# Turning transfers in attention: query block outermost in `probs` and `pT`, 4 KB runs, four partition groups in turn

## What is computed

```python
def attn(x, ...):                      # x: (1, 2048, 256), 16 heads of 128
    q = x @ (wq_codes * repeat(wq_scales, 32)) + bq      # k, v likewise, to 2048 features
    scores = einsum('bqhd,bkhd->bhqk', q, k) / sqrt(128)
    attn = softmax(scores, axis=-1)
    out = einsum('bhqk,bkhd->bqhd', attn, v)
    return out @ (wo_codes * repeat(wo_scales, 32)) + bo
x = x + layernorm(attn(layernorm(x), ...))
x = x + layernorm(experts(layernorm(x), ...))
```

## Time and profile before

| | us |
|---|---|
| median of 3 runs (lowest, highest) | 2091.43 (2089.87, 2092.95) |
| the profiled execution | 2085.26 |
| its span, first to last instruction | 2083.5 |
| TensorE busy | 1966.5 (94%) |
| VectorE busy | 1750.0 (84%) |
| GpSimd busy | 1525.5 (73%) |
| ScalarE busy | 1417.0 (68%) |
| mean granted TensorE clock | 0.975 of full speed |
| transfers `pT<-probs` | 2032 of 128 KB, 2.3 us to landing in the median |

### The profile page before, as it was taken

How to read it: one execution, slowest core, us unless ns; L and a number is a source line. 1 busy time by engine, 2 the same in 40 slices (tenths; PEclk the granted TensorE clock), 3 DMA queues, 4 the chain that set the end, 5 groups by cost and what they waited for, 6 DMA issues and landing times.

```text
span 2083.5 us, 33186 instructions
## 1 busy us (share of the span) xinstructions
PE 1966.5 (94%) x10902; PEld 1697.1 (81%) x10902; DVE 1750.0 (84%) x2706; ACT 1417.0 (68%) x2686; POOL 1525.5 (73%) x1317
## 2 busy tenths in 40 slices
PE   6999999999999999999999999999999999976882
PEld 5888888888888888888888888888888888865772
DVE  7889889998989888988999898988898898976444
ACT  5777767776777767776777667776777667762444
POOL 2679778887778777977888777977787787973222
PEclk9999999999999999999999999999999999986996
DMA  4667757786767767775767666765677566842443
GB/s 103 158 154 185 177 143 175 176 184 149 169 163 182 164 146 171 176 166 134 167 156 175 151 152 156 179 158 138 161 175 165 137 157 147 205 107 75 131 127 104
DMA packets 238064, 322.66 MB, mean 155 GB/s; under 512 B 47686, under 2 KB 105798, under 8 KB 237894
## 3 DMA queue, kind: packets, MB, share of 16 engines
q1 hardware_dynamic: 234822, 312.15, 63.4%
q0 software_dynamic: 3072, 8.39, 1.3%
HBM read 35.68 MB, written 18.35 MB: 26 GB/s over the span
## 4 chain that ended last, share of the span: by engine, by line
PE 69%; SPq 10%; POOL 6%; ACT 4%; DVE 4%; issue 3%; DMA 2%; another core or an unknown queue 0%; POOLq 0%; ACTq 0%
PE ps_a L749 16%; PE ps_s L621 12%; PE ps_s L622 11%; PE ps_s L623 11%; SPq L395 9%; PE ps_a L750 8%; POOL pT_both L518 5%; PE ps_a L621 3%; PE ps_a L623 3%; PE ps_a L622 3%; ACT probs L1037 2%; DVE part_max L1393 1%; DMA pT<-probs 1%; ACT pT_both L1054 1%; POOL x_rows L594 1%
## 5 line engine op out<-in xcount | busy, mean ns | idle before, releaser
L518 POOL TENSOR_TENSOR pT_both<-pT,pT_both 128x512 fp32r<-128x512 f32 x1016 | 1289.3, 1298 | 342.2 <-ACT pT_both L1054 340.6
L749 PE MATMUL ps_a<-pT_both,v_both 128*128 128x512 f32 x2048 | 743.8, 397 | 1.2 <-POOL pT_both L518 1.2
L1037 ACT ACTIVATE probs<-ps_s,shift 128x1024 f32<-128x1024 f32 x512 | 565.9, 1108 | 259.2 <-DVE shift L1402 258.9
L1054 ACT ACTIVATE pT_both<-pT 128x512 fp32r<-128x512 f32 x1016 | 605.7, 629 | 189.2 <-DMA pT<-probs 157.9
L1418 DVE STREAM_TRANSPOSE probs<-probs 128x1024 f32<-128x1024 f32 x508 | 614.2, 1229 | 58.3 <-ACT probs L1037 57.7
L1393 DVE TENSOR_REDUCE part_max<-ps_s 128x1 f32<-128x1024 f32 x512 | 612.0, 1214 | 19.9 <-PE ps_s L623 18.4
L750 PE MATMUL ps_a<-pT_both,v_both 128*128 128x256 f32 x2048 | 573.9, 280 | 0.0
L749 PEld LDWEIGHTS ps_a<-pT_both,v_both 128*128 128x128 f32 x2048 | 385.3, 188 | 86.6 <-POOL pT_both L518 1.1
L621 PE MATMUL ps_s<-kT_hi,qT_hi 128*128 128x512 f32 x1024 | 406.3, 397 | 15.3 <-ACT probs L1037 12.1
L622 PE MATMUL ps_s<-kT_lo,qT_hi 128*128 128x512 f32 x1024 | 402.9, 393 | 0.0
L623 PE MATMUL ps_s<-kT_hi,qT_lo 128*128 128x512 f32 x1024 | 401.3, 392 | 0.0
(11 more groups left out here) (202 smaller groups left out, 2584.5 us busy)
## 6 DMA issues: line engine op xcount, KB each, us to landing
pT<-probs SPq DMA_DIRECT2D x2032, 128.0 KB, 2.3
x_rows<-zeros SPq DMA_DIRECT2D x46, 128.0 KB, 2.2
xg<-x_rows SPq DMA_DIRECT2D x46, 128.0 KB
y_rows<-y_sb SPq DMA_DIRECT2D x46, 128.0 KB
pT<-in_L_attn_x SPq DMA_DIRECT2D x4, 512.0 KB, 5.7
codes<-in_L_attn_wk_codes SPq DMA_DIRECT2D x16, 128.0 KB, 2.4
scales<-in_L_attn_wk_scales SPq DMA_DIRECT2D x64, 32.0 KB, 3.0
codes<-in_L_attn_wo_codes SPq DMA_DIRECT2D x16, 128.0 KB, 2.3
```

What stands on the lines that cost most here:

```text
L518: pool.tensor_tensor(pT_lo[:, p, :].rearrange("p (i n) -> p i n", i=Q4), pT[:, s % 2, g, :, t:t + 2, :].rearrange("p i t q -> p i (t q)"), ...
L749: nc.tensor.matmul(out_both, v_hi[:, h % 2, k, :], move, start=k == 0, stop=False)
L1037: nc.scalar.activation(out, src, ACT.Exp, bias=shift[:, s % SLOTS, r:r + 1], scale=SCALE, accum_out=sums[:, s % SLOTS, r, g:g + 1])\
L1054: nc.scalar.activation(pT_hi[:, p, :].rearrange("p (i n) -> p i n", i=Q4), pT[:, s % 2, g, :, t:t + 2, :].rearrange("p i t q -> p i (t q)" ...
```

## The change

The index of the block of 32 becomes the outermost in `probs` and in `pT`. In `probs` the order in a partition goes from (g, j, t, r, q) to (j, g, t, r, q), and in `pT` from (g, i, t, q) to (i, g, t, q), where i is the block of 32 queries and j the block of 32 keys within a tile. What a transfer takes from a partition of `probs` and puts into one of `pT` was two runs of 2 KB, one for each g, and is now one of 4 KB. The loops that issue the 16 transfers change too: before, the source group stayed for four transfers while the destination went over the four groups; now four transfers in a row take the sources 0 to 3 and the destinations (i + k) mod 4. The patterns of those that read and write the two tensors follow. The transpose's blocks no longer lie at one distance (j and t can't be joined), so its pattern has one dimension more.

```diff
-        pT = sb("pT", [P, 2, NG2, Q4, GT, RH * 32], f32, att)
+        pT = sb("pT", [P, 2, Q4, NG2, GT, RH * 32], f32, att)
...
-            return probs[:, s % 2, :].rearrange("p (g j t r q) -> p g j t r q", g=NG2, j=Q4, t=GT, r=RH)[:, g]
+            return probs[:, s % 2, :].rearrange("p (j g t r q) -> p j g t r q", j=Q4, g=NG2, t=GT, r=RH)[:, :, g]
...
-                for i in range(Q4):
-                    for b in range(Q4):
-                        src = probs[32 * i:32 * (i + 1), s % 2, :].rearrange("p (g j n) -> p g j n", g=NG2, j=Q4)
-                        dst = pT[32 * b:32 * (b + 1), s % 2, :, i, :, :].rearrange("p g t q -> p g (t q)")
-                        sp.dma_start(dst, src[:, :, b, :]).then_inc(pT_loaded[s % 2], 16)
+                for k in range(Q4):
+                    for i in range(Q4):
+                        b = (i + k) % Q4
+                        src = probs[32 * i:32 * (i + 1), s % 2, :].rearrange("p (j n) -> p j n", j=Q4)[:, b, :]
+                        dst = pT[32 * b:32 * (b + 1), s % 2, i].rearrange("p g t q -> p (g t q)")
+                        sp.dma_start(dst, src).then_inc(pT_loaded[s % 2], 16)
...
-                                   pT[:, s % 2, g, :, t:t + 2, :].rearrange("p i t q -> p i (t q)"),
+                                   pT[:, s % 2, :, g, t:t + 2, :].rearrange("p i t q -> p i (t q)"),
...
-                                     pT[:, s % 2, g, :, t:t + 2, :].rearrange("p i t q -> p i (t q)"),
+                                     pT[:, s % 2, :, g, t:t + 2, :].rearrange("p i t q -> p i (t q)"),
...
-                tile = blocks(w % NH, g)[:, :, :, r, :].rearrange("p j t q -> p (j t) q")
+                tile = blocks(w % NH, g)[:, :, :, r, :]
```

More of the change, by code:

```diff
@@ L124, in sandwich_layer @@
         scales = sb("scales", [P, 2, P], f32, att)
-        x_in = pT[:, 0].rearrange("p g i t q -> p (g i t q)").rearrange("p (t d) -> p t d", d=D)
-        xn_in = pT[:, 1].rearrange("p g i t q -> p (g i t q)").rearrange("p (t d) -> p t d", d=D)
+        x_in = pT[:, 0].rearrange("p i g t q -> p (i g t q)").rearrange("p (t d) -> p t d", d=D)
+        xn_in = pT[:, 1].rearrange("p i g t q -> p (i g t q)").rearrange("p (t d) -> p t d", d=D)
         first_codes = {k: probs[:, 0, 4 * P * n:4 * P * n + 2 * P].rearrange("p (c n) -> p c n", c=2)
```

## The result

| | before | after |
|---|---|---|
| median, 11 runs of each side by side | 2091.81 us | 2087.05 us |
| lowest to highest | 2088.51 to 2094.27 | 2083.85 to 2090.33 |
| ratio, 95% interval | | 0.9976 [0.9968, 0.9984] |
| span of the profiled execution | 2083.5 us | 2084.1 us |

The account below looks back on a forecast made before the run. The prediction took attention to be bound by TensorE's matmuls, with 9.0 us of waits. It summed 7.5 us there and 1.5 at its end to 9.0, taken off the median 2091.43: 2082.4 us, range 2073 to 2096.

Parts of the forecast that it names:

- Attention can give back at most 9.0 us; 7.5 of them go: TensorE's waits from 100 to 1800 us total 9.0 us; cheaper turning transfers were to remove 7.5 of them.
- The waits for `oT_lo`: Two TensorE waits in attention, 1.5 us, for VectorE's work, expected to be late next and to stay.
- 0.05 us less for each issue: SyncE's issue of a turning transfer at L395 was to get 0.05 us cheaper, with 0 to 0.27 as range.
- The data need 0.57 us and are the floor: DMA engines at full share need 0.57 us for 128 KB, the floor that SyncE's queue of turning transfers can reach.
- The queue has no slack in a stretch, so 64 issues add up: SyncE's queue is just over its limit in some stretches; 64 issues at 0.05 us less give 3.2 us.
- The end of attention, 1.5 us: Last two turning groups follow one another uncovered: 32 issues at 0.05 us save 1.6 us, 1.5 with some lost.
- VectorE's transpose, ScalarE, GpSimd at no cost; the order worth nothing: Transpose L1418, exponentials, rounding and remainder keep their times; the new order leaves the data rate unchanged.
- The signs: L395 about 545 ns, groups 9.4 us, TensorE's waits under 2 us, last group done near 1819, L1418 near 1229 ns.
- the saving in a stretch: In attention, four back-to-back groups on SyncE's queue, 64 issues at 0.05 us less, were to save 3.2 us.
- the likeliest case: Whole kernel: the forecast case alone, with chance 0.45, was to take 2079 to 2087 us.

Follow-up runs that it names:

- e10: Changed kernel with the last four of the 16 turning transfers of a step left out: 2080.63 us, 0.993 of before.
- e11: Changed kernel with the last head's value-bias product made at step 7 of head 14 instead of step 5: 2083.16 us, 0.9947 of before.
- e4: Changed kernel with each turning transfer cut to its first 2 KB of a partition, 64 KB each: 2081.78 us, 0.9951 of before.
- e8: Each turning transfer copies 128 KB as 128 partitions of 1 KB to the same partitions: 2063.3 us in one run, beside 2068.56 of before.
- e5: Changed kernel with the scales of a head's weights loaded in fewer, larger transfers: 0.9981 of before.
- e6: Changed kernel with one more 128 KB transfer of zeros behind the turning group in each of the last 74 steps: 0.9984 of before.
- e2: Kernel before with only the new order of issue, in the old layout: 0.9999 of before.
- e1: New layout with 4 KB runs alone, issued in the old order: 0.9975 of before.
- e12: Changed kernel once more, beside three others on the same chip: 2086.07 us, 0.9956 of before.
- e3: Changed kernel once more, beside the two halves of the change: 0.9962 of before.
- e9: Changed kernel with an additional transfer of zeros in front of the turning group in each of the last 74 steps: 2090.57 us, 0.9979 of before.

## Why the prediction was right or wrong

- *Attention can give back at most 9.0 us; 7.5 of them go.* The bound held, as did reading it from TensorE's waits. But 2.1 us were a wait for the value bias (e10, e11), and of the 6.9 that hang on transfers the change took 4.3. The waits for `oT_lo`, which I took for what is late next, belonged to the transfers.
- *0.05 us less for each issue.* The mis-sized term. The pairs of two runs and one that I took it from the earlier trace rows were right for the first issue of a group, which gained 0.073. But I read the 585 ns after a pause as proof that nothing holds the queue up. Something does from the second issue on: 0.634 us from one to the next, where 0.555 follow a first one. Fifteen of sixteen issues gained 0.006. It was 0.16 us for a group, not 0.8.
- *The data need 0.57 us and are the floor.* The floor is another, at 0.63, and it isn't the data's (e4, e8).
- *The queue has no slack in a stretch, so 64 issues add up.* The wrong step. A queue that issues without pause for 50 us looked like the cause. It was busy and had slack: 3.6 us less for a head didn't help (e5), 47 us more in all cost at most a few (e6). What counts is one chain in a pair of heads with 32 of those issues, and with GpSimd's and the weights' share, which I had not followed back, and it counts only where it is over some 38.1 us.
- *The end of attention, 1.5 us.* By the group's 0.16 us it is 0.3. The traces can't confirm it: the two groups of the earlier trace rows took 12.42 and 12.17 us and now take 10.24 and 10.02, but a group without a long issue took 10.2 before as well, so nearly all of that is long issues of one execution. For the same reason the last group's end, at 1824.3 and not 1828.9 us, isn't the change's alone.
- *VectorE's transpose, ScalarE, GpSimd at no cost; the order worth nothing.* All as forecast (L1418 and e2). The transpose's slack is 1.6 us for four of them, so it is 0.4 us each and not the 0.3 written there; nothing hangs on it.
- *The signs.* L395 was to fall to 545 ns, a group to 9.4 us, TensorE's waits under 2 us and the last group to end near 1819. It is 591 ns, 10.0 us, 4.7 us and 1824.3: the first three show the cheaper issue, and each far less of it.

Two errors worked against each other: the saving in a stretch was 3.2 us by my sum and is 0.64 (four groups at 0.16), and it was then cut off by a bound that was nearly right. That the forecast came within a factor of two is in part luck of that kind. With 0.33 to 0.6 us for a chain and a stall behind four of the seven, the sum would have been 1.3 to 2.4 us in attention and 0.3 behind it: about 2089 to 2090. The measured 4.8 us are more. All seven chains would give 4.5 at most, and how much of the rest comes with the change and how much with where the long issues fall stays open. The range held no change at all (2091) as well as the forecast, so that it held says little; the likeliest case, 2079 to 2087, was missed by a hair.

## What to carry to other kernels

A queue that never pauses isn't a bound until work taken off it makes something faster. Follow the chain of waits back from each stall to the step where it has slack, and count the change only as often as it stands in there, and only where the chain is longer than that slack. And before a cheaper issue is multiplied by the number of issues, look at the second one in a row: the first may show its own cost and the others the pace of the queue.

## What the runs showed of the hardware that I had not expected

- Transfers within SBUF follow each other on SyncE's queue at 0.633 to 0.644 us from start to start, whether they carry 64 or 128 KB, on 32 partitions or on 128 (e4, e8). What sets that pace stays open.
- Single issues take much longer, most of them 1 to 2.3 us; some 70 from 100 to 1800 us take over 0.8. In the changed kernel 69 of 70 overlap a packet of 16 KB on the queue that the page lists as "instruction" (89 packets in all, about one in 23 us). It reads like SyncE waiting for its own program, which no run here tested. Where such a packet falls in the chain it costs 1 to 1.4 us, and twice in one chain in the rows above; as the table of the seven pairs shows, that goes far to decide whether TensorE stalls there, and it is one reason why executions of one kernel differ.
- A long stall can cost more than itself. In the changed kernel TensorE stood 2.10 us until 1672.76, and its granted clock was at half (1.2 GHz) from 1672.7 for 3.4 us, a mean of 0.59 in this stage:

```profile
1672.00:1676.00 4.00, 3.24 (x8) 2.59 (x9) 2.38 (x5) 3.72 (x8) 2.97 (x3) 0.59 0.92 209
```

  The same stall was followed by it in e1, e10 and e12 too, and not in the profiled executions of before and of e3; in e9 it came behind three of the stalls.
